# Attention with a mixture-of-experts gate on one core: expert groups cut in half, one per step and ahead of the value matmuls, fewer transfers per head group, weights and biases staged later

## The chip, the cores and the metric

The kernel runs on one core of a Trainium2 chip. The metric is the device time of one execution in microseconds (us); lower is better. The state before is given as the median of three runs. All durations below come from one profiled execution of it.

## What is computed

`x` is 4 sequences of 1024 tokens with 128 features, in float32. After a layer norm the same rows feed two branches, whose product is added to `x`:

```python
xn = _layernorm(x, axis=-1)
s = _L0_attn_ref(xn, Wv, bv, Wo, bo)     # q = k = v = xn @ Wv.T + bv, 16 heads of 8
g = _silu(_L0_ffn_ref(xn, ...))          # second norm, router, top 2 of 8 experts, 128 -> 256 -> 128
x = x + s * g
```

In the attention q, k and v are the same projection, the softmax runs over 1024 keys, and the scale is 1/sqrt(8). In the second branch every token goes to the two experts with the highest router logits (`gelu`, exact form) and the two results are mixed with renormalised weights.

## The kernel before, in words

Every engine has its instructions written out in order; semaphores tie the engines together. The program has a front part, 256 steps, and a short tail.

**Front part.** The 4096 tokens are 32 tiles of 128, in 8 blocks of 4 tiles. VectorE (DVE) makes the norm's statistics (`norm1`, L684 and on), ScalarE (ACT) applies them (L592), TensorE (PE) transposes each block (`turn_x`, L1020), projects it (L1027), makes router logits (L1032), transposes the projection back for the values (`turn_p`, L1040) and sums squares per head (L1046). GpSimd (POOL) splits the projection into a high and a low part (L532 to L537), and the DMA queue of SyncE (SP) stores both parts in `p_dram` (L390) and half the squared norm in `m_dram` (L392). At the end of the front part a branch on the largest norm chooses whether an exact path runs; with these inputs it doesn't.

**The steps.** A unit is 4 heads of one sequence; there are 16 units of 16 steps. A step g is one block of 128 keys against 512 queries, for 4 heads: PE makes the scores in two halves of two heads (L1096, into three PSUM pairs in turn), ACT takes the exponential of each half (L651), and two steps later (`VLAG`) PE multiplies them with the values (L1108) into one PSUM bank, `bank_v`, which collects 8 steps. After each 8 steps, at g = 1 mod 8, `turn_out` on DVE waits for the last value matmuls, transposes `bank_v` (L908), which frees it for the next 8 steps, and then divides by the row sums (L911, L912). `k_ring` and `q_ring` hold the operands of two units; SP loads a unit with 20 transfers (L375 to L383).

**The other work.** Everything else that PE does during the steps goes through one further PSUM bank, `bank_f`: each user ("use") writes it on PE (`write_bank`), and DVE reads it (`read_bank`) before the next use may write. PE waits for `bank_f_read` ahead of a use. The table `USES`, made by `timetable()`, says at which step each use stands: a "turn" and a "project" for each unit (attention output transposed at L1121, output projection L1125), two counts of the router, 40 "up" uses (L1140) and 40 "down" uses (L1150). The experts' tokens are sorted into 80 groups of 128 rows (40 for each half of the tokens, `h`). A quad is four groups; a use holds two groups of a quad, so four 128x128 matmuls. In a step the uses stand last:

```python
scores(g, 0); scores(g, 1)
if g >= VLAG: values(g - VLAG)
for use in USES.get(g, []): write_bank(*use)
```

DVE's order in a step is `turn_out` (where due), the reads of this step's uses, then `beside(g)`: router arithmetic, the transposes of expert inputs (`turn_z`, L888), the mixing (`combine`, L893, L895) and the last products (L902, L903). POOL issues the indirect transfers that scatter the rows to `z_dram` (L548) and gather the results (L564), and stores `o_ring` (L554). SP loads weights into rings of two quads (`load_w1` L440, `load_w2` L451) and the sorted rows (L462) in the order of the step numbers, and waits in that order. The exact gelu (L631) runs once for each half of the tokens on ACT, at the steps `GELU_AT`; the uses of the first two down quads stand together in the step of it ("burst").

The expert work stands at steps 31 to 189, mostly one use in every second step.

Of the kernel before, what the change touches and what calls it, by code (L numbers as in the profile page):

```python
# [16 lines left out]
P = 128  # L17
B, S, D = 4, 1024, 128
H = 16
# [36 lines left out]
KQ_LOADS = PART_LOADS + 4  # L56
XC = 8
# [15 lines left out]
ROUTE_AT = (0, 16)  # L73
SCALE_Z_AT = (5, 22)
EXP_AT = (2, 18)
COUNT_AT = (7, 23)
WEIGH_AT = (13, 29)
SCALE_W1_AT = 10
SCATTER_AT = (13, 30)
MOE_AT = 31  # L80
MOE_STEP = 2.1
GATHER_LAG = 3
COMBINE_LAG = 5


def timetable():
# [15 lines left out]
    def both(kind, q, t):  # L102
        for i in range(2):
            t = max(t, place((kind, q, i), t) + 1 - MOE_STEP) + MOE_STEP
        return t

    def burst(first, t):

        g = int(t) + 2
        while g in uses:  # L110
            g += 1
        uses[g] = [("down", first + k, i) for k in range(2) for i in range(2)]
        at.update({what: g for what in uses[g]})
        return g

    for h in range(HALVES):
        place(("count", h), COUNT_AT[h])
    t = MOE_AT
# [6 lines left out]
    for k in range(2, QUADS):  # L125
# [4 lines left out]
    for k in range(2, QUADS):  # L130
# [7 lines left out]
    gather = [at["down", (h + 1) * QUADS - 1, 1] + GATHER_LAG for h in range(HALVES)]  # L138
# [5 lines left out]
SILU_AT = (GATHER_AT[0] + HT + COMBINE_LAG + 2, min(GATHER_AT[1] + HT + COMBINE_LAG + 2, STEPS))  # L144
# [4 lines left out]
def build(nc, x, Wv, bv, Wo, bo, ln_g, ln_b, rW, rb, W1, b1, W2, b2, out):  # L149
    ctx = ExitStack()  # L150
    with ctx:
# [98 lines left out]
        p_dram = nc.dram_tensor("p_dram", [H, PARTS, DK, N], F32)  # L250
        w1_dram = nc.dram_tensor("w1_dram", [E, P, W1W], F32)
        w2_dram = nc.dram_tensor("w2_dram", [E, P, W2W], F32)
        m_dram = nc.dram_tensor("m_dram", [MPARTS, H, N], F32)
# [3 lines left out]
        x_in = [sem(f"x_in{c}") for c in range(NT // XC)]  # L257
# [44 lines left out]
        w2_kept = sem("w2_kept")  # L302
        logits_mm = sem("logits_mm")
# [38 lines left out]
        def _(sp):  # L342
            def load_x(c):
                sp.dma_start(x_tok[:, c * XC:(c + 1) * XC, :], x_v[:, c * XC:(c + 1) * XC, :]).then_inc(x_in[c], 16)
# [9 lines left out]
            for c in range(1, NT // XC):  # L354
                load_x(c)
            sp.dma_start(rb_bc[:, :], rb.rearrange("(a d) -> a d", a=1).broadcast_to([P, E])).then_inc(small_in, 16)
            sp.dma_start(bo_bc[:, :], bo.rearrange("(a d) -> a d", a=1).broadcast_to([P, D])).then_inc(small_in, 16)
            sp.dma_start(w1_stage, W1.rearrange("e h f -> h e f")).then_inc(w1_staged, 16)
            for c in range(FC):
                sp.dma_start(w2_dram[:, :, c * D:(c + 1) * D], W2[:, c * P:(c + 1) * P, :]).then_inc(w2_kept, 16)  # L360
            for e in range(E):
                sp.dma_start(w2_dram[e, :, FC * D:W2W], b2[e:e + 1, :].broadcast_to([P, D])).then_inc(w2_kept, 16)
            sp.wait_ge(zeros_ready, 1)
            sp.dma_start(m_dram[1, :, :], s_tok[0:H, :, :].rearrange("h t d -> h (t d)")).then_inc(m_zeroed, 16)
# [6 lines left out]
            def load_heads(batch, first_head, slot, loaded):  # L371
                for j in range(4):
                    head = p_dram[bass.ds(first_head + j, 1), :, :, bass.ds(batch * S, S)].rearrange("h a d n -> (h a d) n")
                    first = 32 * j
                    sp.dma_start(k_ring[first:first + DK, slot, :].bitcast(F32), head[0:DK, :]).then_inc(loaded, 16)  # L375
                    sp.dma_start(k_ring[first + DK:first + 3 * DK, slot, :].bitcast(F32), head[:, :]).then_inc(loaded, 16)
                    sp.dma_start(q_ring[first:first + 2 * DK, slot, :].bitcast(F32), head[:, :]).then_inc(loaded, 16)
                    sp.dma_start(q_ring[first + 2 * DK:first + 3 * DK, slot, :].bitcast(F32), head[0:DK, :]).then_inc(loaded, 16)

            def load_stabiliser(n, loaded):  # L380
                for j in range(4):
# [806 lines left out]
```

## Time and profile before

| what | value |
|---|---|
| median of 3 runs | 669.34 us (668.44 to 671.91) |
| the profiled execution | 668.3 us, its span 666.6 us |
| PE matmul busy | 585.1 us (88%), weight load 247.6 us |
| ACT busy | 540.7 us (81%), of it L651: 480.0 us in 512 instructions |
| DVE busy | 222.5 us (33%) |
| POOL busy | 171.3 us (26%) |
| DMA | 77.15 MB, mean 116 GB/s |
| first exponential, last exponential | at 74.4 us, at 656.1 us |

Busy shares are averages over three stages: a front part of 74 us, 582 us of steps, and a tail. An engine that is 88% busy in the mean can be the limit in one stretch and idle for 13 us in another, so the stretches are read apart below. The granted clock of TensorE is one of two levels, 1.2 or 2.4 GHz, shown as tenths of full speed.

### The profile page before, as it was taken

What the parts mean: (1) busy time and instruction counts of PE and PEld (TensorE: products, weight loads), DVE (VectorE), ACT (ScalarE), POOL (GpSimd) and SP (SyncE); (2) the same over time, 40 slices, a digit from 0 to 9 for tenths busy, and PEclk for the clock granted to TensorE, in tenths of its full rate; (3) what the DMA queues carried; (4) which work ended last, traced back from release to release, by engine and by line L of the source; (5) the groups of instructions that cost most, each with busy time, mean ns of one, the idle gap of its engine ahead of it and who ended that gap; (6) DMA issues with size and microseconds to landing.
All of it is one profiled execution on the core that took longest, in us unless ns stands there. A gap on an engine that the chain in (4) does not pass through costs nothing.

```text
span 666.6 us, 11435 instructions
## 1 busy us (share of the span) xinstructions
PE 585.1 (88%) x4002; PEld 247.6 (37%) x4002; DVE 222.5 (33%) x581; ACT 540.7 (81%) x595; POOL 171.3 (26%) x192
## 2 busy tenths in 40 slices
PE   1895599929897997999999999979979899699996
PEld 1673123213343444344444444344434332223231
DVE  5942556613232321222222231224415123321111
ACT  3533599918586889889888989898888799999995
POOL 5435007777600000000000000547300067300000
PEclk9958599959898996999999999969979899989998
DMA  7628335444754453555544453445725241312000
GB/s 217 159 73 301 96 153 165 113 102 137 180 134 110 97 114 97 122 135 137 130 111 122 124 133 91 131 124 148 190 82 160 88 102 52 89 33 58 1 10 8
DMA packets 96212, 77.15 MB, mean 116 GB/s; under 512 B 52723, under 2 KB 86918, under 8 KB 95622
## 3 DMA queue, kind: packets, MB, share of 16 engines
q1 hardware_dynamic: 90454, 62.73, 35.8%
q0 software_dynamic: 5696, 13.64, 7.0%
q8 instruction: 33, 0.54, 0.3%
q14 instruction: 29, 0.24, 0.1%
HBM read 53.77 MB, written 24.13 MB: 117 GB/s over the span
## 4 chain that ended last, share of the span: by engine, by line
PE 60%; ACT 14%; issue 9%; SPq 7%; DMA 4%; DVE 4%; POOL 2%; POOLq 0%; ACTq 0%; DVEq 0%
PE bank_v L1108 27%; PE pair L1096 14%; ACT exps L651 12%; PE bank_f L1150 7%; PE bank_f L1140 6%; POOL rows_in_sb L564 2%; SPq L439 1%; PE bank_f L1125 1%; DVE o_turned L908 1%; DMA rows_in_sb<-o_dram,dest_i 1%; DMA m_dram<-pre 1%; SPq L440 1%; DMA bo_bc<-in_L_attn_bo 1%; SPq L462 1%; PE pair L1027 1%
## 5 line engine op out<-in xcount | busy, mean ns | idle before, releaser
L651 ACT ACTIVATE exps<-pair 128x1024 f32<-128x1024 f32 x512 | 480.0, 1080 | 78.2 <-PE pair L1096 76.7
L1108 PE MATMUL bank_v<-exps,v_tok 128*32 128x512 f32 x2048 | 283.8, 627 | 5.7 <-DVE o_turned L908 3.3
L1096 PE MATMUL pair<-q_ring,k_ring 26*128 26x512 f32 x1024 | 176.5, 514 | 14.5 <-ACT exps L651 8.9
L1096 PEld LDWEIGHTS pair<-q_ring,k_ring 26*128 26x128 f32 x1024 | 76.2, 188 | 177.6 <-ACT exps L651 112.5
L554 POOL DMA_DIRECT2D o_dram<-o_ring x20 | 15.4, 768 | 292.2 <-DVE o_ring L950 288.7
L548 POOL DMA_INDIRECT z_dram<-pre,dest_i x64 | 63.4, 990 | 49.2 <-DVE dest_i L871 30.0
L1108 PEld LDWEIGHTS bank_v<-exps,v_tok 128*32 128x32 f32 x2048 | 41.9, 110 | 72.9 <-issue 56.9
L564 POOL DMA_INDIRECT rows_in_sb<-o_dram,dest_i x64 | 60.8, 950 | 25.5 <-issue 20.1
L1140 PE MATMUL bank_f<-zT,w_ring 128*128 128x128 f32 x320 | 48.5, 298 | 21.3 <-issue 13.2
L1150 PE MATMUL bank_f<-w_ring,pre 128*128 128x128 f32 x320 | 52.8, 315 | 10.8 <-ACT pre L631 5.2
L1140 PEld LDWEIGHTS bank_f<-zT,w_ring 128*128 128x128 f32 x320 | 40.8, 200 | 56.0 <-issue 45.1
L1150 PEld LDWEIGHTS bank_f<-w_ring,pre 128*128 128x128 f32 x320 | 44.5, 216 | 42.2 <-issue 29.6
L941 DVE TENSOR_TENSOR pre<-bank_f,w_ring 128x512 f32<-128x512 f32 x40 | 27.6, 690 | 92.1 <-PE bank_f L1140 92.1
L908 DVE STREAM_TRANSPOSE o_turned<-bank_v 128x512 f32<-128x512 f32 x32 | 22.9, 717 | 103.2 <-PE bank_v L1108 103.0
L950 DVE TENSOR_TENSOR o_ring<-bank_f,w_ring 128x256 f32<-128x256 f32 x40 | 17.0, 424 | 108.2 <-PE bank_f L1150 108.2
L592 ACT ACTIVATE xn_tok<-x_tok,shift,rstd 128x128 f32<-128x128 f32 x32 | 13.0, 480 | 9.5 <-DVE shift L691 9.5
L888 DVE STREAM_TRANSPOSE zT<-z_ring 128x512 f32<-128x512 f32 x20 | 14.2, 710 | 16.2 <-DMA z_ring<-z_dram 15.6
L631 ACT ACTIVATE pre<-pre 128x2048 f32<-128x2048 f32 x10 | 18.2, 1896 | 0.0
L613 ACT ACTIVATE pre<-bank_v 16x512 fp32r<-16x512 f32 x8 | 4.7, 586 | 16.5 <-PE bank_v L1046 9.6
L893 DVE SCALAR_TENSOR_TENSOR xn_tok<-rows_in_sb,weight,xn_tok 128x128 f32<-128x128 f32 x32 | 11.3, 352 | 15.9 <-DMA rows_in_sb<-o_dram,dest_i 15.6
L1020 PE MATMUL pair<-ident,xn_tok 128*128 128x128 f32 x32 | 8.4, 415 | 8.8 <-ACT xn_tok L592 8.8
L926 DVE TENSOR_TENSOR s_tok<-bank_f,bo_bc 128x256 f32<-128x256 f32 x16 | 6.8, 424 | 27.5 <-PE bank_f L1125 27.5
(129 smaller groups left out, 296.1 us busy)
## 6 DMA issues: line engine op xcount, KB each, us to landing
w_ring<-w_dram SPq DMA_DIRECT2D x80, 192.0 KB
w_ring<-w_dram SPq DMA_DIRECT2D x80, 129.0 KB
z_dram<-s_tok SPq DMA_DIRECT2D x4, 1280.0 KB, 6.6
z_ring<-z_dram SPq DMA_DIRECT2D x80, 64.0 KB, 2.4
o_dram<-o_ring POOLq DMA_DIRECT2D x20, 256.0 KB, 3.2
p_dram<-pre SPq DMA_DIRECT2D x16, 256.0 KB, 3.2
k_ring<-p_dram SPq DMA_DIRECT2D x64, 64.0 KB
q_ring<-p_dram SPq DMA_DIRECT2D x64, 64.0 KB
```

The lines of the kernel that those rows point to most:

```text
L548: pool.indirect_dma_start(z_dram[h][:, :], bass.IndirectOffsetOnAxis(dest_i[:, h, c, i:i + 1].bitcast(U32), 0), z0[:, h * HT + i, :], None ...
L554: pool.dma_start(o_dram[h][k * 4 * P:(k + 1) * 4 * P, :].rearrange("(a p) d -> p a d", p=P), o_ring[:, q % 2, :, :]).then_inc(o_stored[q % ...
L564: pool.indirect_dma_start(rows_in_sb[:, (h * HT + i) % GATHER_RING, c, :], None, o_dram[h][:, :], bass.IndirectOffsetOnAxis(dest_i[:, h, c ...
L631: nc.scalar.activation(part, part, ACT.Gelu).then_inc(gelu_done, 1)
L651: nc.scalar.activation(exps[:, g % ES, 2 * half:2 * half + 2, :], pair[(2 * g + half) % 3][:, :, :], ACT.Exp, scale=SCALE).then_inc(exp_do ...
L908: nc.vector.transpose(o_turned[:, qh, :, :], bank_v[:, :].rearrange("p (r s) -> p s r", s=QR)).then_inc(o_turned_ready, 1)
L941: ins = nc.vector.tensor_tensor(pre[:, k, i * BLK:(i + 1) * BLK].rearrange("p (s c t) -> p s c t", s=2, c=FC), bank_f[:, :].rearrange("p ( ...
L950: ins = nc.vector.tensor_tensor(o_ring[:, q % 2, 2 * i:2 * i + 2, :], bank_f[:, 0:2 * D].rearrange("p (a d) -> p a d", a=2), w2_ring[:, q ...
L1096: ins = nc.tensor.matmul(pair[h % 3][:, j % 2, :], k_ring[32 * j:32 * j + KROWS, n % 2, kt * P:(kt + 1) * P], q_ring[32 * j:32 * j + KROWS ...
L1108: ins = nc.tensor.matmul(bank_v[32 * j:32 * j + 32, :], v_tok[:, (n // HG) * KT + kt, first:first + 32], exps[:, g % ES, j, :], start=(kt ...
L1140: ins = nc.tensor.matmul(bank_f[:, at * P:(at + 1) * P], w1_ring[:, q % 2, a, c * P:(c + 1) * P], zT[:, q % 2, a * P:(a + 1) * P], start=T ...
L1150: ins = nc.tensor.matmul(bank_f[:, (a % 2) * D:(a % 2 + 1) * D], pre[:, k, (a * FC + c) * P:(a * FC + c + 1) * P], w2_ring[:, q % 2, a, c ...
```

## The change

It does eight things.

- A use holds one group: two matmuls in place of four. There are 160 expert uses, up and down, with a new table; outside the bursts nearly every step from 31 to 217 has one. A burst has eight.
- In a step that has exactly one use, PE now writes it between the scores and the value matmuls. In a burst it still comes last. This holds for turn, project and count too.
- `p_dram` holds for each head the rows high, high, low, high, norm, zero (two of them filled by a copy in DRAM at step 2), so that a unit from the third on is loaded with 8 transfers, not 20. The first two units are loaded as before; the first unit's loads are spread over four blocks.
- The 16 small bias matmuls of W1 leave the front part and become four "bias" uses at steps 4 to 7.
- PE does 9 and 8 matmuls of the identity into `bank_v` ahead of the first block (`keep_warm`). The norm's first chunks are smaller, and DVE keeps block 0's values ahead of the last chunk. The loads of `rb` and `bo` aren't waited for there any more.
- The zeroing of `z_dram` moves behind the branch (first half) and to step 16 (second half); the copy of W2 and b2 into DRAM moves from the start to step 24 of SP's queue.
- The router arithmetic and the scatter stand earlier: the first scatter at step 6 (13 before), the second at 22 (30 before).
- `store_o` moves from POOL's queue to SP's, and `combine` takes 7 steps for 5 tiles in place of 5.

```diff
-ROUTE_AT = (0, 16)
-SCALE_Z_AT = (5, 22)
-COUNT_AT = (7, 23)
-SCALE_W1_AT = 10
-SCATTER_AT = (13, 30)
+RANK_AT = ((0, 0, 1, 1, 2, 2), (13, 14, 15, 16, 18, 19))
+COUNT_AT = (3, 20)
+ASSIGN_AT = ((3, 4, 4, 5, 6), (21, 22, 23, 24, 26))
+SCALE_Z_AT = ((3, 4, 5, 6), (14, 15, 16, 18))
+BIAS_AT = 4
+SCALE_W1_AT = (8, 10, 11, 12)
+SCATTER_AT = (6, 22)
 MOE_AT = 31
-MOE_STEP = 2.1
+MOE_STEP = 1.12
...
     def both(kind, q, t):
-        for i in range(2):
+        for i in range(4):
...
             def load_unit(n):
                 if n >= 2:
                     sp.wait_ge(pv_done, (n - 1) * US)
-                load_heads(n // HG, (n % HG) * 4, n % 2, kq_in[n % 2])
-                load_stabiliser(n, kq_in[n % 2])
+                if n == 2:
+                    sp.wait_ge(hi_copied, 32)
...
+                    sp.dma_start(k_ring[32 * j:32 * j + PROWS, n % 2, :].bitcast(F32), p_dram[head, 0:PROWS, tokens]
+                                 ).then_inc(kq_in[n % 2], 16)
+                    sp.dma_start(q_ring[32 * j:32 * j + KROWS, n % 2, :].bitcast(F32), p_dram[head, HI_ROW:HEAD_ROWS, tokens]
+                                 ).then_inc(kq_in[n % 2], 16)
...
+            zero_z(0)
             load_unit(1)
-            zero_z(1)
...
+                if g == SCATTER_AT[1] - 6:
+                    zero_z(1)
+                if g == SCATTER_AT[1] + 2:
+                    keep_w2()
                 for q in range(HALVES * QUADS):
-                    if g == (TURN_Z_AT[q - 2] + 1 if q >= 2 else SCATTER_AT[0] + HT - 1):
+                    if g == (TURN_Z_AT[q - 2] + 1 if q >= 2 else MOE_AT - 3):
                         load_z(q)
-                    if g == (AT["up", q - 2, 1] + 1 if q >= 2 else SCATTER_AT[0] + 9 + q):
+                    if g == (AT["up", q - 2, 3] + 1 if q >= 2 else MOE_AT - 8 + 2 * q):
                         load_w1(q)
...
-            norm1(0, 0, XC)
+            norm1(0, *NORMS[0])
+            norm1(1, *NORMS[1])
             router_weights()
-            norm1(1, XC, XC)
-            norm1(2, 2 * XC, 2 * XC)
+            norm1(2, *NORMS[2])
             keep_p(0)
+            norm1(3, *NORMS[3])
+            keep_p(1)
+            keep_p(2)
...
-                    for a in range(2 * i, 2 * i + 2):
-                        for c in range(FC):
-                            at = (a % 2) * FC + c
-                            ins = nc.tensor.matmul(bank_f[:, at * P:(at + 1) * P], w1_ring[:, q % 2, a, c * P:(c + 1) * P],
-                                                   zT[:, q % 2, a * P:(a + 1) * P], start=True, stop=True)
+                    for c in range(FC):
+                        ins = nc.tensor.matmul(bank_f[:, c * P:(c + 1) * P], w1_ring[:, q % 2, i, c * P:(c + 1) * P],
+                                               zT[:, q % 2, i * P:(i + 1) * P], start=True, stop=True)
...
+                ahead = len(USES.get(g, [])) == 1
+                if ahead:
+                    write_bank(*USES[g][0])
                 if g >= VLAG:
                     values(g - VLAG)
-                for use in USES.get(g, []):
-                    write_bank(*use)
+                if not ahead:
+                    for use in USES.get(g, []):
+                        write_bank(*use)
```

How rows move, on PE. Steps 41 and 42 of the program; L1140 (before) and L1191 (now) write the expert uses, L1096 and L1142 the scores, L1108 and L1154 the value matmuls. Before, from the scores of step 41:

```order
L1096 MATMUL pair<-q_ring,k_ring 128x512 x4
L1108 MATMUL bank_v<-exps,v_tok 32x512 x4
L1140 MATMUL bank_f<-zT,w_ring 128x128 x4
L1096 MATMUL pair<-q_ring,k_ring 128x512 x4
L1108 MATMUL bank_v<-exps,v_tok 32x512 x4
```

Now, from the second use of the two, with the semaphores:

```order
L1191 MATMUL bank_f<-zT,w_ring 128x128
L1154 MATMUL bank_v<-exps,v_tok 32x512 [waits exp_done]
L1154 MATMUL bank_v<-exps,v_tok 32x512 x3
L1142 MATMUL pair<-q_ring,k_ring 128x512 [waits exp_done]
L1142 MATMUL pair<-q_ring,k_ring 128x512
L1142 MATMUL pair<-q_ring,k_ring 128x512 [waits exp_done]
L1142 MATMUL pair<-q_ring,k_ring 128x512
L1191 MATMUL bank_f<-zT,w_ring 128x128 [waits bank_f_read]
L1191 MATMUL bank_f<-zT,w_ring 128x128
L1154 MATMUL bank_v<-exps,v_tok 32x512 [waits o_turned_ready,exp_done]
L1154 MATMUL bank_v<-exps,v_tok 32x512 x3
```

The last value matmuls of an 8-step block now stand behind step 41's use and ahead of step 42's, which waits for `bank_f_read`; before, step 42 had no use.

On DVE, around the same place. L888 and L926 are `turn_z`, L908 to L912 and L946 to L950 `turn_out`, L941 and L981 the reads of the up uses. Before:

```order
L888 STREAM_TRANSPOSE zT<-z_ring 128x512
L941 TENSOR_TENSOR pre<-bank_f,w_ring 128x512
L908 STREAM_TRANSPOSE o_turned<-bank_v 128x512
L911 RECIPROCAL rden<-o_turned 128x16
L912 TENSOR_TENSOR attn<-o_turned,rden 128x128
L941 TENSOR_TENSOR pre<-bank_f,w_ring 128x512
L888 STREAM_TRANSPOSE zT<-z_ring 128x512
```

Now:

```order
L926 STREAM_TRANSPOSE zT<-z_ring 128x512
L946 STREAM_TRANSPOSE o_turned<-bank_v 128x512
L949 RECIPROCAL rden<-o_turned 128x16
L950 TENSOR_TENSOR attn<-o_turned,rden 128x128
L981 TENSOR_TENSOR pre<-bank_f,w_ring 128x256 x4
L926 STREAM_TRANSPOSE zT<-z_ring 128x512
```

The reads are half as wide and twice as many, and in both the read of the use of step 41 stands behind the three instructions of `turn_out`.

## Rows read from the trace of the kernel before

**Rows 1.** Chain of work that ended last, late steps: start us, us, what.

```profile
592.08 1.67 ACT exps L651 x2
593.88 1.70 ACT exps L651 x2
```

**Rows 2.** Timeline, PE, two expert uses: start us, us, engine, line, operation.

```profile
303.75 1.16 PE L1150 MATMUL bank_f<-w_ring,pre 128*128 128x128 f32 x8
304.84 0.51 PE L1096 MATMUL pair<-q_ring,k_ring 26*128 26x512 f32 x4
305.28 1.06 PE L1108 MATMUL bank_v<-exps,v_tok 128*32 128x512 f32 x8
306.28 0.69 PE L1096 MATMUL pair<-q_ring,k_ring 26*128 26x512 f32 x4
307.89 1.16 PE L1150 MATMUL bank_f<-w_ring,pre 128*128 128x128 f32 x8
```

**Rows 3.** Groups by form: scatter; timeline: what waited for it.

```profile
L548 POOL DMA_INDIRECT z_dram<-pre,dest_i x64 | 63.4, 990 | 49.2 <-DVE dest_i L871 30.0 <-issue 19.2
...
145.57 0.71 DVE L888 STREAM_TRANSPOSE zT<-z_ring 128x512 f32<-128x512 f32 x1 [15.60 <-DMA z_ring<-z_dram]
```

**Rows 4.** Waits, 150 to 250 us: us in total, times, longest us.

```profile
PE bank_f L1140 <- DMA w_ring<-w_dram: 7.9, 3, 3.5
```

**Rows 5.** Page, part 2: granted clock of PE in 40 slices, tenths.

```profile
PEclk9958599959898996999999999969979899989998
```

**Rows 6.** Timeline, PE, a project use (two matmuls) and the scores after it.

```profile
609.27 0.71 PE L1125 MATMUL bank_f<-woT,attnT 128*128 128x128 f32 x4
609.91 0.51 PE L1096 MATMUL pair<-q_ring,k_ring 26*128 26x512 f32 x4
```

**Rows 7.** Timeline at the end of 8 steps; last, groups by form, a 256-wide read.

```profile
170.69 1.16 PE L1140 MATMUL bank_f<-zT,w_ring 128*128 128x128 f32 x8
170.90 0.72 DVE L908 STREAM_TRANSPOSE o_turned<-bank_v 128x512 f32<-128x512 f32 x1 [2.45 <-PE bank_v L1108]
172.15 0.68 DVE L941 TENSOR_TENSOR pre<-bank_f,w_ring 128x512 f32<-128x512 f32 x1
...
L926 DVE TENSOR_TENSOR s_tok<-bank_f,bo_bc 128x256 f32<-128x256 f32 x16 | 6.8, 424 | 27.5 <-PE bank_f L1125 27.5
```

**Rows 8.** Timeline, PE, second and third down use of the first burst.

```profile
257.86 2.08 PE L1150 MATMUL bank_f<-w_ring,pre 128*128 128x128 f32 x8 [0.52 <-DVE o_ring L950]
260.52 2.08 PE L1150 MATMUL bank_f<-w_ring,pre 128*128 128x128 f32 x8 [0.59 <-DVE o_ring L950]
```

**Rows 9.** Timeline, SP's queue: W2 and b2 copied to DRAM at the start.

```profile
9.49 6.41 SPq L360 DMA_DIRECT2D w_dram<-in_L_ffn_W  x2
...
15.94 7.42 SPq L362 DMA_DIRECT2D w_dram<-in_L_ffn_b  x8
```

**Rows 10.** Chain of work that ended last, front part.

```profile
31.95 4.99 PE bank_f L1011 x32
...
59.59 6.88 DMA m_dram<-pre
```

**Rows 11.** Timeline, PE, sum of squares of four blocks: two slow turns, two fast.

```profile
42.42 0.60 PE L1046 MATMUL bank_v<-pre,head_sel 128*16 128x512 bf16 x1
...
48.15 0.60 PE L1046 MATMUL bank_v<-pre,head_sel 128*16 128x512 bf16 x1
...
52.57 0.38 PE L1046 MATMUL bank_v<-pre,head_sel 128*16 128x512 bf16 x1
...
55.61 0.38 PE L1046 MATMUL bank_v<-pre,head_sel 128*16 128x512 bf16 x1
```

**Rows 12.** Timeline, DVE: norm of the last 16 tiles, and what follows it.

```profile
19.76 3.19 DVE L684 BATCH_NORM_STATS2 rows_in_sb<-x_tok 128x6 f32<-128x128 f32 x16
...
29.07 0.69 DVE L707 COPY v_tok<-pair 128x512 f32<-128x512 f32 x1
```

**Rows 13.** Groups by form: one of the router's wide comparisons.

```profile
L808 DVE TENSOR_TENSOR pre<-pre 128x1024 bf16<-128x1024 f32 x2 | 2.4, 1222 | 0.0
```

More of the change, by code:

```diff
@@ L111, in burst @@
             g += 1
-        uses[g] = [("down", first + k, i) for k in range(2) for i in range(2)]
+        uses[g] = [("down", first + k, i) for k in range(BURST) for i in range(4)]
         at.update({what: g for what in uses[g]})
@@ L117, in timetable @@
         place(("count", h), COUNT_AT[h])
+    for part in range(4):
+        place(("bias", part), BIAS_AT + part)
     t = MOE_AT
@@ L124, in timetable @@
     t = both("up", QUADS + 1, t)
-    for k in range(2, QUADS):
+    for k in range(BURST, QUADS):
         t = both("down", k, t)
@@ L129, in timetable @@
     t = gelu[1] + 4
-    for k in range(2, QUADS):
+    for k in range(BURST, QUADS):
         t = both("down", QUADS + k, t)
@@ L137, in timetable @@
             order[what] = len(order)
[L138 removed]
+    gather = [at["down", (h + 1) * QUADS - 1, 3] + GATHER_LAG for h in range(HALVES)]
     return uses, at, order, gelu, gather
@@ L476, in _ @@
                     load_unit(n + 1)
-                if g == SCALE_W1_AT + 6:
+                if g == 2:
+                    for row in (0, LO_ROW + DK):
+                        sp.dma_start(p_dram[:, row:row + DK, :], p_dram[:, HI_ROW:HI_ROW + DK, :]).then_inc(hi_copied, 16)
+                if g == SCALE_W1_AT[-1] + 1:
                     sp.wait_ge(w1_scaled, 1)
@@ L571, in _ @@
                         scatter(h, g - SCATTER_AT[h])
-                for q in range(HALVES * QUADS):
-                    if g == AT["down", q, 1] + 1:
-                        store_o(q)
                 for h in range(HALVES):
@@ L681, in norm1 @@
                 for t in range(count):
-                    if (first + t) % XC == 0:
-                        dve.wait_ge(x_in[(first + t) // XC], 16)
+                    for chunk, (start, _) in enumerate(X_CHUNKS):
+                        if first + t == start:
+                            dve.wait_ge(x_in[chunk], 16)
                     ins = nc.vector.bn_stats(stats[:, t, :], x_tok[:, first + t, :])
@@ L782, in scale_w1 @@
                     dve.wait_ge(w1_staged, 16)
-                    dve.wait_ge(biases_mm, 1)
+                    dve.wait_ge(bank_f_written, written("bias", 3))
                 some = slice(2 * part, 2 * part + 2)
@@ L928, in read_bank @@
                                                   bo_bc[:, :].unsqueeze(1).broadcast_to([P, UT, D]), ALU.add)
+                elif what == "bias":
+                    some = slice(arg[0] * 4, arg[0] * 4 + 4)
+                    ins = nc.vector.tensor_tensor(b1p[:, some], bank_f[:, 0:4], cols[:, some], ALU.add)
                 elif what == "count":
@@ L996, in _, with keep_warm @@
             pe.wait_ge(consts_ready, 8)
+            def keep_warm(count):
+                for _ in range(count):
+                    nc.tensor.matmul(bank_v[:, 0:P], ident[:, :], ident[:, :], start=True, stop=True)
+            keep_warm(WARM[0])
             pe.wait_ge(rows_in, 16 * 6)
@@ L1126, in write_bank @@
                                                start=True, stop=True)
+                elif what == "bias":
+                    if arg[0] == 0:
+                        pe.wait_ge(w1_staged, 16)
+                    for at in range(4):
+                        e, c = divmod(arg[0] * 4 + at, FC)
+                        ins = nc.tensor.matmul(bank_f[:, at:at + 1], w1_stage[:, e, c * P:(c + 1) * P],
+                                               cols[:, E * FC + 1:E * FC + 2], start=True, stop=True)
                 elif what == "count":
```

234 lines of the change are left out of this document (124 added, 110 removed).

## The prediction

> **What bounds the kernel now.** I read the page first for the clock, then the chain of waits, then timelines of single steps, because the busy shares average over stretches with different limits. Late in the run, where no expert work is left, the chain stays on ACT and a pair of exponentials starts every 1.80 us [rows 1]: ACT bounds those steps at 1.81 us. Where expert uses stand in every second step, PE bounds. Two steps take 307.89 - 303.75 = 4.14 us, and the timeline splits them: the use 1.09, scores 0.44, values 1.00, scores again up to the next use 1.61 with values [rows 2]. So a step with a whole use costs PE 0.44 + 1.00 + 1.09 = 2.53, a step without one 1.44, below ACT's 1.81; together the pair loses 4.14 - 3.61 = 0.53 us against ACT. Between steps 31 and about 60 the limit is neither: PE stands at its queue's head for sorted rows or weights [rows 3, 4]. The granted clock falls to the lower of its two levels (1.2 GHz) in the front part, after the gap for the rows and at both gelus, the slices with 5 or 6 tenths [rows 5].
>
> **The sum, part by part.** It is made against the profiled execution's 668.3 us; the median of the runs shown is 1.0 higher. All terms are changes of that time.
>
> *Half uses.* Two fp32 matmuls of 128x128 into `bank_f` are what a project use is: 609.91 - 609.27 = 0.64 us [rows 6]. A step with a half use then takes PE 0.44 + 0.64 + 1.00 = 2.08, which is 0.27 over ACT's 1.81. Outside the bursts there are 144 half uses: 144 x 0.27 = 39. Before there were 72 whole ones at 0.53: 38. So cutting the groups in half brings nothing by itself, because the fixed part of a use, 2 x 0.64 - 1.09 = 0.19, is paid twice and eats what the better balance gives. Term: 0. Bounds: no row shows a use between scores and values. At 0.55 (half of 1.09) it would be -13, at 0.73 +13. I take 0.64, the row with the same shape.
>
> *The place ahead of the values.* This is the largest loss. At g = 1 mod 8 DVE has to do `turn_out` before it reads that step's use. `turn_out` waits for the value matmuls, which now stand behind the use. After the values end on PE (170.69) the transpose starts 0.21 later, and the read of the use 1.46 later; a read 256 wide takes 0.42 [rows 7]; with 0.06 for the semaphore (what the 0.58 between two burst uses leaves beside read and its start [rows 8]) PE may write the next use 1.94 us after the values' end. PE has only the scores of the next step, 0.44, to do meanwhile, and its own value matmuls are queued behind the waiting use, the next scores behind those, and ACT behind the scores. So it stands for 1.5 us. With the use behind the values, scores and values (1.44) and the use of the step before (0.64) would have covered it. In the new table 21 ends of 8 steps have one use in both steps. At three of them (steps 49, 97, 137) a `turn_z` of 0.71 [rows 3] follows that read, and the next use, the first of its quad, waits for it too. 21 x 1.5 + 3 x 0.7 = +33.6. What it gives back: the value matmuls that open a new 8 steps waited for the transpose (0.21 + 0.72 + 0.06 after the end, scores cover 0.44: 0.55) where a use made PE late, in 8 steps before: -4. ACT has 0.27 to spare a step in this stretch, but it is PE that is late, so nothing is recovered.
>
> *Bursts.* Each use there waits for the read of the one before: start to start 260.52 - 257.86 = 2.66, of which 0.58 is the handshake, at the lower clock [rows 8]. Eight half uses take 8 x (1.04 + 0.5) = 12.3, four whole ones 10.6. PE already finished after the gelu, so the end shows: +1.7 to +2.6 twice, +4.5.
>
> *The scatter.* First use before: POOL issues 32 indirect transfers for half the tokens at (63.4 + 19.2) / 64 = 1.29 us each, 41 us; DVE waited 15.6 us for sorted rows, and PE and ACT behind it [rows 3]. Now it starts about 7 steps (12.6 us) earlier, and step 31 comes some 3 us later, so the rows come in time by POOL. But SP's queue is passed differently: W2's and b2's copy stands at step 24, between the W1 loads and the rows' loads. [...] Behind it are four W1 loads and the row loads. I leave 4 us of stall: -11. Bounds: -15 (copy hidden), 0 (SP as late as POOL was).
>
> *Weight waits.* PE waited three times for W1, 7.9 us in all [rows 4], each time with a unit's 20 transfers ahead of the loads on SP, and PE's matmuls behind two of them run at the lower clock. Eight transfers take less than half. With the slow steps behind the waits I put this at -12; bounds -15 and -3 (three waits become short ones). `store_o` on SP adds one issue for each quad; there is room.
>
> *Front part.* The 32 records of the bias matmuls, 4.99 us, leave the chain, and so does the 6.88 us wait for a store that stood behind the zeroing of `z_dram` [rows 10]. A loop over a block took 5.73 us at the lower clock and 3.04 at the higher [rows 11], and the clock fell during the bias matmuls. Against that, DVE now takes block 0's values ahead of the last 16 tiles' norm, 29.07 - 19.76 = 9.3 us of work [rows 12]. The block's sum of squares is there at 26 to 28.6 us by its own loops, so blocks 4 to 7 start at 37 to 40 us, with PE idle before them, in place of about 37 with PE busy (42.42 less a loop). Term -8, bounds -13 and +4. The trace shows the loops up to 51 us at 1.2 GHz, behind the thinly loaded bias matmuls, and those from 52 us at 2.4 [rows 11]. The Trainium skill (TensorE: Matmul & The Clock Gate, What's actually happening) says the default state is throttled and activity releases it; by that the extra identity matmuls bring the higher level sooner, and with it kept for all blocks the term would be -13. The gap ahead of block 4 speaks against its being kept.
>
> *First steps.* Steps 0 to 8 now hold all of the first routing and four bias uses. The wide comparisons are 1.22 us each [rows 13]; with the routing's small ones I estimate 2.4 us of DVE work a step against 1.81. PE waits at the count and bias uses: +3 (0 to +6).
>
> *Late stretch.* Slower gathering (7 steps for 5 tiles) avoids DVE waits ahead of reads, and a step behind a free one has 0.2 us in hand: -4 (0 to -6). The gathers of the second half start at step 220 and have 36 steps, 65 us, for 41 us of POOL's work, so the tail stays. Nothing for the 8-transfer units beyond the above: bytes are equal.
>
> Sum: 0 + 33.6 - 4 + 4.5 - 11 - 12 - 8 + 3 - 4 = +2 us, so 670 by the profiled run. I take 669, as the gains' bounds reach a little further than the losses'.
>
> **Rivals.**
>
> 1. *The wait at the end of 8 steps is mostly covered.* If DVE's read came soon enough, or most of these places found PE early, half of the 33 us goes: about 650. For it: only DVE timings of before stand behind the 1.94. Against: no use was written there before, and the order on both engines is fixed. 0.15.
>
> 2. *A use ahead of the values costs less.* If its weights are loaded while the scores still stream, only the pieces are left, (1.09 - 0.64) / 4 = 0.11 each, 0.45 in all: 144 x 0.19 = -27, about 642. The trace speaks against it: each change between forms leaves a gap, and the step's 0.64 has it [rows 2, 6]. The Trainium skill (TensorE: Matmul & The Clock Gate, Step-by-step: what each phase is for) has the queue pull weight loads ahead of matmuls in flight where row groups don't conflict. 0.08.
>
> 3. *Slower: SP's queue.* If the copy at step 24 keeps SP beyond step 31, the first rows and the second W1 quad come late, PE idles over 3 us, and its clock falls. It decides from about 10 us for the copy. With the full 13.8 us the stall is about as long as before [rows 3, 9]: +11 and +4 for the clock, about 684. 0.15.
>
> 4. *Slower: the handshake shows in all steps.* Uses in every step leave DVE one step for the read and everything beside it. If `beside` delays reads by 0.3 us in most steps, 144 x 0.3 = +43, about 710. Against: DVE is 33% busy. 0.05.
>
> **How the numbers follow.** My case has 0.57, with bounds of its own terms from 659 to 681; a third of it is over 0.5% faster (about what a measurement of this kernel can tell from no change), a third within, a third slower. Faster: 0.19 + 0.15 + 0.08 = 0.42; same 0.19; slower 0.19 + 0.15 + 0.05 = 0.39. The range leaves out the far ends of rivals 2 and 4: 650 to 686.
>
> **What would show it.** In the profile after: steps with a half use 2.08 us apart; at steps 42, 50, 58, ... 3.6 us, with PE's weight load of the use waiting about 1.5 us for DVE's read of the use before; some 21 such waits. The scatter's wait of 15 us gone and at most 5 us at step 31; no wait over 1 us for W1; first exponential at 66 us (61 to 78). Bursts of about 12 us. I am wrong if step 42 and its like take 2.1 us, if half uses run at 1.9 us, or if SP issues the first row loads later than step 31.

## The result, and the profile after

The changed kernel takes 689.41 us (median of 4 runs, 689.14 to 696.62), the kernel before, run beside it, 670.62 us (4 runs, 668.44 to 674.79). The ratio is 1.0298, with an interval from 1.0213 to 1.0384: slower, and above the forecast range. The profiled execution took 689.35 us with a span of 687.4, so 20.8 us of span have to be found. Where one execution took over 1.5% longer than the fastest of its kernel, the ratio leaves it out; that is one number below, the 660.3 of the first experiment.

A step's length is read here as the distance between the first exponential of one step and of the next, and its excess as what it has over ACT's 1.81 us. Summed by stretch, the excess of the two profiled executions differs as below. Two rows are made otherwise: the ends of 8 steps are what the changed kernel's 21 steps take over a usual step with a use (2.07), and "all else" is what is left of the difference.

| stretch | term of the prediction | measured |
|---|---|---|
| up to the first exponential (74.4 before, 70.9 now) | -8 | -3.5 |
| steps 3 to 8 | +3 | +13.1 |
| steps 9 to 30 | 0 | +0.4 |
| step 31, first sorted rows | -11 | -7.1 |
| 21 ends of 8 steps | +33.6 | +33.3 |
| the two gelus with their bursts | +4.5 | +5.1 |
| the two silus (ACT, L671), five steps each | none | +1.6 |
| all else from step 32 on: 0 for half uses, -4 value waits, -12 weights, -4 late stretch | -20 | -22.1 |
| sum | +2 | +20.8 |

The page of the profile after, cut to its first line, the clock of part 2 (tenths, 40 slices) and one of the costliest groups (busy us, mean ns, idle before and who released it):

```profile
PE 592.3 (86%) x4036; PEld 245.9 (36%) x4036; DVE 238.0 (35%) x677; ACT 547.6 (80%) x595; POOL 155.1 (23%) x172
...
PEclk9677559979999997699999999999789989999977
...
L1191 PE MATMUL bank_f<-zT,w_ring 128*128 128x128 f32 x320 | 58.3, 306 | 25.1 <-DVE pre L981 14.8
```

Before, the low tenths of the clock stood at the front, behind the gap at step 31 and at the gelus [rows 5]; now slices 5 and 6 (69 to 103 us) are low as well, where the first steps run. And the up uses now have a wait that they had not: PE stood 14.8 us for DVE's read of the use before.

**One end of 8 steps.** The timeline of the program's step 42 (start us, us; PEld is the weight load), from the last value matmuls of the old 8 steps:

```profile
173.01 1.06 PE L1154 MATMUL bank_v<-exps,v_tok 128*32 128x512 f32 x8
174.01 0.51 PE L1142 MATMUL pair<-q_ring,k_ring 26*128 26x512 f32 x4
174.15 0.72 DVE L946 STREAM_TRANSPOSE o_turned<-bank_v 128x512 f32<-128x512 f32 x1 [1.86 <-PE bank_v L1154]
174.90 0.25 DVE L949 RECIPROCAL rden<-o_turned 128x16 f32<-128x16 f32 x1
175.18 0.29 DVE L950 TENSOR_TENSOR attn<-o_turned,rden 128x128 f32<-128x128 f32 x1
175.39 0.42 DVE L981 TENSOR_TENSOR pre<-bank_f,w_ring 128x256 f32<-128x256 f32 x1
175.87 0.52 PEld L1191 LDWEIGHTS bank_f<-zT,w_ring 128*128 128x128 f32 x4 [1.67 <-DVE pre L981]
175.87 0.71 PE L1191 MATMUL bank_f<-zT,w_ring 128*128 128x128 f32 x4 [1.35 <-DVE pre L981]
176.51 1.06 PE L1154 MATMUL bank_v<-exps,v_tok 128*32 128x512 f32 x8
177.50 0.19 PEld L1142 LDWEIGHTS pair<-q_ring,k_ring 26*128 26x128 f32 x4 [0.84 <-issue]
...
178.05 1.94 ACT L686 ACTIVATE exps<-pair 128x1024 f32<-128x1024 f32 x2 [1.56 <-PE pair L1142]
```

The transpose starts when the values have ended, the read (L981) comes third behind it, and PE, with only 0.5 us of scores left to do, waits 1.35 us. Behind it stand the value matmuls, behind those the next scores, and ACT waits 1.56 us for them. Most other steps with a use are 2.05 to 2.08 us long. Of the 21 with this wait 18 take 3.36 to 3.57, two 4.19 and 4.20, where `turn_z` follows, and step 50, where `turn_z` follows too and the clock fell, 5.76. (Step 178, without a use in the step before it, takes 3.07 and isn't one of them.) Before, the same place had the transpose, a whole read and no use behind it [rows 7].

**Step 31.** SP's queue, then DVE, and PE:

```profile
128.00 2.33 SPq L377 DMA_DIRECT2D w_dram<-in_L_ffn_W  x2
130.38 8.09 SPq L379 DMA_DIRECT2D w_dram<-in_L_ffn_b  x8
139.68 3.65 SPq L468 DMA_DIRECT2D w_ring<-w_dram  x4
143.37 6.75 SPq L490 DMA_DIRECT2D z_ring<-z_dram  x12
...
147.48 0.71 DVE L926 STREAM_TRANSPOSE zT<-z_ring 128x512 f32<-128x512 f32 x1 [9.04 <-DMA z_ring<-z_dram]
...
148.30 1.19 PE L1191 MATMUL bank_f<-zT,w_ring 128*128 128x128 f32 x4 [6.12 <-issue]
```

The copy at step 24 held SP for 10.5 us, the second W1 quad another 3.7, and so the row loads were first issued at 143.37, behind the start of step 31 (about 142). The step took 9.9 us, where the wait for rows had been 15.60 [rows 3]. In the kernel before the same copy took 6.41 + 7.42 us [rows 9].

**Steps 4 to 7.** PE, two of the four bias uses (L1178), with scores and values:

```profile
80.37 0.80 PE L1142 MATMUL pair<-q_ring,k_ring 26*128 26x512 f32 x4
81.10 1.87 PE L1178 MATMUL bank_f<-cols,w_ring 128*128 128x1 f32 x8
82.90 1.93 PE L1154 MATMUL bank_v<-exps,v_tok 128*32 128x512 f32 x8
84.76 0.80 PE L1142 MATMUL pair<-q_ring,k_ring 26*128 26x512 f32 x4
85.49 1.86 PE L1178 MATMUL bank_f<-cols,w_ring 128*128 128x1 f32 x8
```

PE's rows lie end to end: nothing waits. But scores take 0.73 and values 1.86 from start to start, where they take 0.44 and 1.00 at 2.4 GHz [rows 2], and the four fp32 matmuls of one column (eight records) cost 1.80. A step is 4.39 us, four times over. The granted clock was at the lower level from 64.3 us to 101.8, so up to the step after the last bias use.

### The profile page after: what moved, and what is told of

It reads as the page before. It is cut to its first block and busy times, and to the rows that moved or that the text cites. A ratio compares the mean times of both kernels' runs of the same rounds, so it can differ in the third digit from the quotient of the medians.

```text
span 687.4 us, 11510 instructions
## 1 busy us (share of the span) xinstructions
PE 592.3 (86%) x4036; PEld 245.9 (36%) x4036; DVE 238.0 (35%) x677; ACT 547.6 (80%) x595; POOL 155.1 (23%) x172
## 5 line engine op out<-in xcount | busy, mean ns | idle before, releaser
L686 ACT ACTIVATE exps<-pair 128x1024 f32<-128x1024 f32 x512 | 487.6, 1049 | 93.7 <-PE pair L1142 77.8
L1154 PE MATMUL bank_v<-exps,v_tok 128*32 128x512 f32 x2048 | 287.2, 634 | 2.3 <-DVE o_turned L946 1.6
L1142 PE MATMUL pair<-q_ring,k_ring 26*128 26x512 f32 x1024 | 157.1, 519 | 14.4 <-ACT exps L686 8.7
L1142 PEld LDWEIGHTS pair<-q_ring,k_ring 26*128 26x128 f32 x1024 | 62.4, 190 | 250.1 <-ACT exps L686 193.3
L1200 PE MATMUL bank_f<-w_ring,pre 128*128 128x128 f32 x320 | 64.8, 331 | 24.3 <-DVE o_ring L990 16.3
L1191 PE MATMUL bank_f<-zT,w_ring 128*128 128x128 f32 x320 | 58.3, 306 | 25.1 <-DVE pre L981 14.8
L946 DVE STREAM_TRANSPOSE o_turned<-bank_v 128x512 f32<-128x512 f32 x32 | 22.9, 717 | 133.3 <-PE bank_v L1154 133.3
L981 DVE TENSOR_TENSOR pre<-bank_f,w_ring 128x256 f32<-128x256 f32 x80 | 33.9, 424 | 97.8 <-PE bank_f L1191 97.8
L1200 PEld LDWEIGHTS bank_f<-w_ring,pre 128*128 128x128 f32 x320 | 48.1, 216 | 46.7 <-DVE o_ring L990 22.7
L990 DVE TENSOR_TENSOR o_ring<-bank_f,w_ring 128x128 f32<-128x128 f32 x80 | 23.2, 291 | 107.8 <-PE bank_f L1200 106.9
L1191 PEld LDWEIGHTS bank_f<-zT,w_ring 128*128 128x128 f32 x320 | 43.1, 195 | 45.9 <-issue 23.2
L1154 PEld LDWEIGHTS bank_v<-exps,v_tok 128*32 128x32 f32 x2048 | 41.6, 110 | 46.6 <-issue 20.9
L627 ACT ACTIVATE xn_tok<-x_tok,shift,rstd 128x128 f32<-128x128 f32 x32 | 13.1, 480 | 12.8 <-DVE shift L727 12.8
L926 DVE STREAM_TRANSPOSE zT<-z_ring 128x512 f32<-128x512 f32 x20 | 14.2, 711 | 9.7 <-DMA z_ring<-z_dram 9.0
L575 POOL TENSOR_TENSOR pre<-pre 128x512 bf16<-128x512 f32 x8 | 8.3, 1041 | 31.5 <-ACT pre L642 25.1
L956 DVE COPY attnT<-bank_f 128x256 f32<-128x256 f32 x16 | 6.8, 425 | 22.2 <-PE bank_f L1167 22.2
```

What stands on the lines that cost most here:

```text
L686: nc.scalar.activation(exps[:, g % ES, 2 * half:2 * half + 2, :], pair[(2 * g + half) % 3][:, :, :], ACT.Exp, scale=SCALE).then_inc(exp_do ...
L926: nc.vector.transpose(zT[:, q % 2, :], z_ring[:, q % 2, :]).then_inc(z_turned, 1)
L946: nc.vector.transpose(o_turned[:, qh, :, :], bank_v[:, :].rearrange("p (r s) -> p s r", s=QR)).then_inc(o_turned_ready, 1)
L981: ins = nc.vector.tensor_tensor(pre[:, k, i * HF:(i + 1) * HF].rearrange("p (c t) -> p c t", c=FC), bank_f[:, 0:HF].rearrange("p (c t) -> ...
L990: ins = nc.vector.tensor_tensor(o_ring[:, q % 2, i, :], bank_f[:, 0:D], w2_ring[:, q % 2, i, FC * D:W2W], ALU.add)
L1142: ins = nc.tensor.matmul(pair[h % 3][:, j % 2, :], k_ring[32 * j:32 * j + KROWS, n % 2, kt * P:(kt + 1) * P], q_ring[32 * j:32 * j + KROWS ...
```

## Experiments

Each was run with a profile and timed against the kernel before on the same chip. Ratios are to the kernel before; the changed kernel stands at 1.0298.

**Uses behind the values again**, all else as changed:

```diff
-ahead = len(USES.get(g, [])) == 1
+ahead = False
```

> Every use stands behind the value matmuls, as before; all else as in the change. Theory A (the wait at the ends of 8 steps): the 21 steps behind such an end fall from 3.4 to 3.6 us (4.2 and 5.8 at three) to about 2.1, the waits of PE for DVE's read of the use before are gone, other steps with a half use stay at 2.07; 689.4 - 33 = 656 us. Theory B (the place costs nothing, half uses in nearly every step are what costs): within 3 us of 689. Should the value matmuls that open 8 steps wait for the transpose again, up to 21 x 0.5 = 10 us come back: 666.

Measured 649.46 us (648.34 to 660.3) against 669.59, ratio 0.9705 (0.9632 to 0.9778): one line turns the loss into a gain. The place of step 42 in this kernel:

```profile
163.44 0.72 DVE L946 STREAM_TRANSPOSE o_turned<-bank_v 128x512 f32<-128x512 f32 x1 [0.23 <-PE bank_v L1154]
...
164.38 1.07 PE L1154 MATMUL bank_v<-exps,v_tok 128*32 128x512 f32 x8
...
165.37 0.71 PE L1191 MATMUL bank_f<-zT,w_ring 128*128 128x128 f32 x4
```

PE comes to that use with its values done, and the read is done too; step 42 takes 2.06 us. From step 32 on the excess falls from 121.1 to 90.2 us, by 31.0, which is about the 33.3 less the small value waits that come back. The other 10 us are not the place itself: step 31 is 2.6 shorter, and steps 3 to 16 together 7.5, because here the bias uses met the higher clock:

```profile
81.64 1.06 PE L1154 MATMUL bank_v<-exps,v_tok 128*32 128x512 f32 x8
82.64 1.05 PE L1178 MATMUL bank_f<-cols,w_ring 128*128 128x1 f32 x8
...
87.47 1.15 PE L1178 MATMUL bank_f<-cols,w_ring 128*128 128x1 f32 x8
88.55 0.80 PE L1142 MATMUL pair<-q_ring,k_ring 26*128 26x512 f32 x4
89.28 1.94 PE L1154 MATMUL bank_v<-exps,v_tok 128*32 128x512 f32 x8
```

The same use takes 0.98 instead of 1.80 from start to start, steps 4 to 6 take 2.42, and at the fourth use the clock falls; steps 8 to 10 are then 2.6 to 2.9 long.

**Which of two steps is to blame.** At an end of 8 steps two steps are involved: g = 1 mod 8 brings `turn_out` and its own use ahead of the last values, g = 2 mod 8 brings the use that waits. One kernel each puts only that step's use behind the values (`VLAG` is 2, `KT` is 8):

```diff
-ahead = len(USES.get(g, [])) == 1
+ahead = len(USES.get(g, [])) == 1 and g % KT != VLAG
```

> As the change, but in the steps g = 2 mod 8, and only there, the use stands behind the value matmuls. Theory A: the same 656 to 666 us as with all uses behind, since the place costs only there. Theory B: 689. If the place costs in every step, this one lies between 689 and the run with all uses behind.

```diff
-ahead = len(USES.get(g, [])) == 1
+ahead = len(USES.get(g, [])) == 1 and g % KT != 1
```

> As the change, but in the steps g = 1 mod 8, and only there, the use stands behind the values. By the chain read from DVE: after the values' end PE has the use (0.64) and scores (0.44) to do and may write the next use at 1.94, so it waits 0.86, not 1.5, in each of 21 places: 689.4 - 21 x 0.64 = 676 us, the steps g = 2 mod 8 at about 2.9. If the wait is something else than the read behind turn_out, 689 or 656.

The first took 673.86 us (10 runs; 1.0062, 1.0031 to 1.0094), the second 674.24 (10 runs; 1.0077, 1.0049 to 1.0106). Each recovers 15 us and leaves the other half; for the second that was forecast, for the first 656 to 666 us had been. In the first, the values that open the new 8 steps wait for the transpose, and the use behind them makes step 43 late too: steps 42 and 43 take 2.64 and 2.30.

```profile
174.70 0.72 DVE L946 STREAM_TRANSPOSE o_turned<-bank_v 128x512 f32<-128x512 f32 x1 [1.86 <-PE bank_v L1154]
...
175.57 1.07 PE L1154 MATMUL bank_v<-exps,v_tok 128*32 128x512 f32 x8 [0.49 <-DVE o_turned L946]
```

In the second the last value matmuls don't stand behind a use of 0.64 us, but the use of step 42 still waits (the row below), and the step takes 2.85.

```profile
173.78 0.71 PE L1191 MATMUL bank_f<-zT,w_ring 128*128 128x128 f32 x4 [0.71 <-DVE pre L981]
```

So the wait is one chain, values, transpose, read, next use, and what counts is how much of PE's work stands between its two ends: scores alone (0.44) in the change, scores and one more piece in these two, scores, values and a use (2.08) when both stand behind.

**Bias uses later.**

```diff
-BIAS_AT = 4
-SCALE_W1_AT = (8, 10, 11, 12)
+BIAS_AT = 9
+SCALE_W1_AT = (13, 14, 15, 16)
```

> The four bias uses stand at steps 9 to 12 (4 to 7 in the change), the scaling of W1 at 13 to 16. Theory C (four thin uses at the lower clock, each 1.8 us, keep that clock down): steps 4 to 8 return to 1.82, the clock rises by about step 5 and the bias uses, then at the higher level, cost 2.4 to 2.5 a step; 689.4 - 10 = 679 us. Theory D (the clock stays down until about 100 us whatever PE does, or DVE's routing work sets those steps): steps 4 to 8 stay over 3 us, less than 3 us gained.

Measured 689.13 us (685.53 to 690.38), ratio 1.0289 (1.022 to 1.0359): a miss, nothing gained. Steps 4 to 8 ran at 1.81 to 1.84, with the clock up at 84 us, but then the steps of the bias uses took 2.27, 3.88, 4.38 and 4.39:

```profile
92.16 1.05 PE L1178 MATMUL bank_f<-cols,w_ring 128*128 128x1 f32 x8
...
95.73 1.05 PE L1178 MATMUL bank_f<-cols,w_ring 128*128 128x1 f32 x8 [1.09 <-DVE b1p L969]
96.71 1.07 PE L1154 MATMUL bank_v<-exps,v_tok 128*32 128x512 f32 x8
97.71 0.80 PE L1142 MATMUL pair<-q_ring,k_ring 26*128 26x512 f32 x4
98.44 1.86 PE L1178 MATMUL bank_f<-cols,w_ring 128*128 128x1 f32 x8
```

The clock was up, two bias uses ran on it, and it fell at 97.7. Of the 3.88 us of step 10, 1.09 are a wait for DVE, whose read stands behind `turn_out`. The loss goes where the uses go, so the crowding of the first steps is not its cause.

**Bias uses with 128 columns.** The same four matmuls multiply a copy of the bias column, repeated 128 times (`b_wide`); DVE reads the first column of each.

```diff
-ins = nc.tensor.matmul(bank_f[:, at:at + 1], ..., cols[:, E * FC + 1:E * FC + 2], ...)
+ins = nc.tensor.matmul(bank_f[:, at * P:(at + 1) * P], ..., b_wide, ...)
```

> As the change, but each of the 16 bias matmuls moves 128 equal columns, not one (column 0 is read); same places, same number of instructions. Theory C (thin matmuls keep the clock down): the clock rises by about step 5, steps 5 to 7 take about 2.5, not 4.39, and 8 to 11 stay at 1.82: 689.4 - 8 = 681 us. Theory G (transfers or the routing keep steps 4 to 7 slow, at 84 to 88% DMA share): the steps stay at 4.4 or grow by the wider matmuls, 689 or more.

```profile
83.78 2.08 PE L1178 MATMUL bank_f<-rows_in_sb,w_ring 128*128 128x128 f32 x8
...
87.59 1.16 PE L1178 MATMUL bank_f<-rows_in_sb,w_ring 128*128 128x128 f32 x8
```

At the lower clock the wide use costs more (2.01 from start to start), but the clock rose at 86.6, within its step, and stayed: 3.81, then 2.52 three times. The excess of steps 3 to 8 is 5.6 us, not 13.3. The whole, 685.63 us (682.38 to 687.6; 1.0221, 1.0166 to 1.0276), can't be told apart from the change by these intervals, and the front part of its profiled execution was 3.4 us longer; the verdict rests on the steps. The other runs bear it out: steps 5 to 7 take 2.51 to 2.53 us in all six kernels with wide bias uses, and 4.39 in all four that have one-column uses there ahead of the values. In the Trainium skill, TensorE: Matmul & The Clock Gate (What's actually happening) says that the throttled state is the default and activity releases it. The sentence alone doesn't tell these two cases apart: TensorE's rows lie end to end in both, and with one-column matmuls among them the clock stayed at 1.2 GHz for four steps, with wide ones it rose in the first.

**W2's copy at step 8 of SP's queue.**

```diff
-if g == SCATTER_AT[1] + 2:
+if g == SCATTER_AT[0] + 2:
     keep_w2()
```

> W2 and b2 are copied to DRAM at step 8 of SP's queue, not 24. Theory E (at step 31 the sorted rows wait for SP's queue, which stands in that copy): the row loads are issued at about 131 us, not 143, step 31 takes about 2 us, not 9.9, the clock stays up; 689.4 - 8 = 681 us. Theory F (the scatter itself is late): step 31 stays over 8 us, no gain.

Measured 682.2 us (681.45 to 685.0), ratio 1.0208 (1.0145 to 1.0271). Step 31 is 2.06 us long; its excess goes from 8.09 to 0.25. That is the whole of the stall, so here SP alone was late: its row loads went out at 131.43, and POOL had issued the last scatter of the first half by 129.8.

**The three together**, behind the values, wide bias, early copy:

> All uses behind the values, the W2 copy at step 8, and the right side of the bias matmuls 128 equal columns wide in place of one (column 0 of each is read). If the three costs are separate: 649.5 - 7 (step 31) - 4 (steps 4 to 11, where the run with all uses behind still had a slow stretch) = 638 us. If they cover one another: no less than 645.

Measured 649.91 us (647.85 to 651.05), ratio 0.9709 (0.9667 to 0.975): no better than the first edit alone (638 had been forecast if the three costs are separate). Step 31 is clean, but step 26 takes 7.88. The copy now holds SP for 23.7 us, and the zeroing of `z_dram`'s second half (L384) stands behind it; DVE's output of the first project waits for it:

```profile
85.81 14.87 SPq L377 DMA_DIRECT2D w_dram<-in_L_ffn_W  x2
100.72 8.82 SPq L379 DMA_DIRECT2D w_dram<-in_L_ffn_b  x8
...
111.12 3.12 SPq L384 DMA_DIRECT2D z_dram<-s_tok  x2
```

and from its waits (us in total, times, longest):

```profile
DVE s_tok L964 <- DMA z_dram<-s_tok: 7.9, 1, 7.9
```

**And the zeroing ahead of the copy** ("mended" from here on):

```diff
-if g == SCATTER_AT[1] - 6:
+if g == 4:
     zero_z(1)
```

> As the run with three mends, and the second half of z_dram is zeroed at step 4 of SP's queue, ahead of the W2 copy. There the copy held back that zeroing, and DVE's read of the first projection waited 7.9 us for it. Without it: 649.9 - 7 = 643 us, no step below 31 over 3 us from step 8 on. If another transfer behind the copy is late instead: 648 to 650.

Measured 648.01 us (6 runs, 646.21 to 650.58), ratio 0.9693 (0.9667 to 0.9718). Step 26 is clean, and the stall is at step 31 again, 7.9 us of excess:

```profile
DVE zT L926 <- DMA z_ring<-z_dram: 10.8, 1, 10.8
```

Step 31 comes sooner, at 132.9 us, by what the earlier stretches saved, and SP is late again, by a third path. SP's queue, a wait of SP in it (us in total, times, longest), and POOL's 32nd scatter, the last that these rows need:

```profile
87.33 20.55 SPq L377 DMA_DIRECT2D w_dram<-in_L_ffn_W  x2
...
116.94 0.74 SPq L517 DMA_DIRECT2D w_dram<-b1p  x1
...
127.32 8.31 SPq L468 DMA_DIRECT2D w_ring<-w_dram  x8
135.68 6.90 SPq L490 DMA_DIRECT2D z_ring<-z_dram  x12
...
SPq L463 <- DMA w_dram<-b1p: 2.4, 1, 2.4
...
128.54 1.08 POOL L592 DMA_INDIRECT z_dram<-pre,dest_i  x1 [0.30 <-issue]
```

The copy now holds SP for 28.9 us. The store of W1's bias behind it lands at 126.2, the eight W1 loads wait for that, and the row loads go out behind them without a wait for POOL. By POOL alone they could have gone out at about 130.9, an estimate from the kernel before, where they did so 1.3 us after the 32nd scatter had ended (140.41 and 141.72). So some 4.8 of the 7.9 us are SP's, and POOL would be the next to be late. That is the other forecast of this run, another transfer behind the copy that is late (648 to 650 us). No run here moves the copy behind the row loads.

**The last 16 tiles' norm ahead of block 0's values**, on the mended kernel:

```diff
-            keep_p(0)
             norm1(3, *NORMS[3])
+            keep_p(0)
```

> As the mended kernel, but DVE makes the norm of the last 16 tiles before it keeps block 0's values, as the kernel before did. In the change, PE stood idle for 5.6 us ahead of block 4, at 38.4 us. If that order is what kept the front part long, block 4 starts at about 31 to 33 us and the first exponential comes 4 to 7 us earlier: 637 us. If the slow clock or the stores set the front part's length: within 2 us of the mended kernel.

Measured 645.73 us (6 runs, 643.24 to 647.46), ratio 0.9649 (0.9619 to 0.9678), the lowest median here and ahead of both kernels; the gain over the mended kernel, 2.3, is less than the 4 to 7 forecast, and the two intervals touch. The first exponential is at 67.5 instead of 71.4, and step 31 gives 1.2 back.

**Twenty transfers for each unit again**, on the mended kernel:

```diff
-KQ_LOADS = 4 * 2
+KQ_LOADS = KQ_FIRST
```

and `load_unit` loads every unit as it loads unit 1.

> As the mended kernel, but each unit is loaded with 20 transfers, as before. If they cause the waits for W1 before: 5 to 13 us slower, with waits of PE for w_ring at steps 38 to 60. If the new table's spacing alone took those waits away: within 2 us.

Measured 656.28 us (6 runs, 655.05 to 656.98), ratio 0.9802 (0.9778 to 0.9825), 8.3 over the mended kernel. Its profiled execution loses 10.4, of it 5.6 in steps 32 to 78, and there PE waits for weights three times, where the mended kernel shows one wait of 1.1:

```profile
PE bank_f L1191 <- DMA w_ring<-w_dram: 3.7, 3, 1.8
```

**Whole groups again**, on the mended kernel, one in every second step:

```diff
-MOE_STEP = 1.12
+MOE_STEP = 2.1
...
-        for i in range(4):
+        for i in range(2):
```

with four matmuls to a use and reads twice as wide, as before.

> As the mended kernel, but with whole uses (two groups, four matmuls) at the places of the kernel before, one in every second step. From the step lengths half uses bring nothing by themselves (144 x 0.27 against 72 x 0.53) and lose about 5 us in the bursts: this run at 636 to 643 us, no more than 3 us from the mended one or a little below. If cutting the groups is a gain: over 650.

Measured 654.01 us (6 runs, 650.09 to 655.89), ratio 0.977 (0.974 to 0.98), 6.0 over the mended kernel: a miss, since at most 3 had been forecast, and over 650 us if cutting the groups is a gain. The steady rate is not the reason: a step without and a step with a whole use take 1.82 + 2.31 = 4.13, two half uses 2 x 2.075 = 4.15. It loses more at single places, the largest a late quad of weights at step 60 (6.51 us long against 3.22 in the mended kernel, with the lower clock in the two behind it):

```profile
PE bank_f L1196 <- DMA w_ring<-w_dram: 2.9, 1, 2.9
```

**The kernel before with its single uses ahead of the values:**

```diff
+ahead = len(USES.get(g, [])) == 1
+if ahead: write_bank(*USES[g][0])
 if g >= VLAG: values(g - VLAG)
-for use in USES.get(g, []): write_bank(*use)
+if not ahead:
+    for use in USES.get(g, []): write_bank(*use)
```

> The kernel before with whole uses, in which a single use of a step is written ahead of the values; nothing else. Theory A: the place costs only where two neighbouring steps around an end of 8 steps have uses; before, that is one place (steps 33, 34 have it not, nearly all ends have one use), and the value matmuls that open 8 steps no longer wait for the transpose, 8 x 0.5: 670 - 4 = 666 us. If the place costs in general: over 680.

Measured 675.77 us (10 runs, 673.13 to 678.94), ratio 1.0088 (1.0055 to 1.0121): a miss, I had expected no loss. With a use in every second step most ends of 8 steps cost little (about 0.25 us at seven of them), and where the opening values had waited for the transpose a step even gained some 0.4 us. But where a use is not ready, matmuls that are ready now stand behind it:

```profile
170.11 2.05 PE L1140 MATMUL bank_f<-zT,w_ring 128*128 128x128 f32 x8 [3.80 <-DMA w_ring<-w_dram]
172.09 1.94 PE L1108 MATMUL bank_v<-exps,v_tok 128*32 128x512 f32 x8
```

Step 39 took 8.44 us, not 4.03, and step 56 10.01, not 6.66. The first of these was got back, since steps 43 to 45 together were 5.0 shorter; of the second 1.1 was. Steps 31, 106 and 114 lost 1.9, 1.0 and 2.1 more. At steps 106 and 114 the use, first of its quad, waited 1.6 for DVE's `turn_z`, which stands behind `turn_out` and so behind the end of the values.

## Why the prediction was wrong

It forecast 669 us and no change; the sum was +2 and 20.8 came. The direction was missed by terms on the side, not by the main one.

- **The step that failed is "First steps: +3 (0 to +6)".** It counted DVE's work and PE's waits, and put PE's own time for the four bias uses, and the clock behind it, at nothing. They took 1.80 us each, and the clock stayed at its lower level through them, which made the scores and values of four steps dearer as well: +13.1. The wait for DVE that I expected is there too, in step 3 alone (3.99 us). The two runs that move and widen the bias uses show the uses themselves as the cause: late ones carry the loss with them, wide ones shed 7.7 of the 13.1 us. I had read the same 32 records in the front part as 4.99 us [rows 10] and had even noted that the clock fell there, and then credited their removal and did not charge their return.
- **"The scatter: -11" was too large; it is -7.1.** The place was right, and rival 3 is its mechanism: the copy held SP for 10.5 us, just over the 10 from which it was to decide, and the first row loads were issued later than step 31, a sign of being wrong that the prediction names. The early copy shows that all of the remaining stall was this. My 4 us were 8.1.
- **"Front part: -8" came to -3.5.** PE stood 5.55 us ahead of block 4, as forecast, behind the last 16 tiles' norm. Moving that norm ahead brought the first exponential 3.9 us forward in one profiled execution and the median down by 2.3, and the higher clock was not kept for all blocks.
- **The silus were left out**, +1.6 us. The first costs 7.5 us of excess in five steps in both kernels (from step 171 before, 197 now). The second costs 7.4 against 5.8; behind it the clock was low for 10.2 us against 6.8. Why, no run shows.
- **The place ahead of the values was right**: +33.6 forecast, +33.3 measured, 3.5 us for step 42, PE waiting 1.35 where I had 1.5. Rival 1 is out. Its removal gave 31.0 us from step 32 on, where 33.6 - 4 = 29.6 follows from the terms.
- **Half uses at 2.08 us** were right, so rivals 2 and 4 are out, and "0" for the cut holds for the steady rate (4.15 against 4.13). But whole groups lose 6.0 us, at single waits, and by the run's own test that is a gain of the cut. That these come from the grouping, and not from how this table happens to fall, isn't shown.
- **Bursts** +5.1 for +4.5; **weights and the rest** -22.1 for -20, and this one is a remainder, not a sum of measured parts. Steps 39, 43 to 45, 56 and 58, the long ones before with W1 late [rows 4], have no counterpart now, and the twenty transfers bring waits of the same kind back.

With 13.1 in place of 3 the forecast would have been about 679 us, within the range; SP's queue (3.9), the front part (4.5) and the silus (1.6) make up the other 10. Open is why the clock was up at the bias uses in the first experiment and not in the change: both have the same work up to step 3 but for the place of the values. The four kernels with the one-column uses of steps 4 to 7 ahead of the values all ran them at the lower level; only one kernel has them behind, profiled once, and that doesn't settle whether it is the order or chance.

## What to carry to other kernels

When a wait is moved into an in-order queue, don't ask how long it is but how much of that engine's ready work stands between the event that starts it and the instruction that waits: here one line that put a use ahead of the value matmuls cut that cover from 2.08 us to 0.44, and taking it back won 31 us. Charge an instruction that is moved for what it did where it stood, its effect on the clock included. And after a stall is removed look for the queue that is late next: this one went from step 31 to step 26 and back to 31, each time behind the same copy in SP's queue and each time by another transfer that stood behind it. Moving the copy earlier made it longer and put more behind it.

## What the runs showed of the hardware

- One-column fp32 matmuls cost far more than their columns. A bias use of four took 0.98 us at 2.4 GHz and 1.80 at 1.2, when an up use, two matmuls of 128 columns, took 0.64 at 2.4 GHz. The granted clock fell behind two such uses that ran at the higher level in one kernel and during the fourth in another, and did not rise in the four kernels where they ran at the lower.
- SP's time for one and the same copy in DRAM (W2 and b2) depends on where it stands: 13.8 us at the start, 10.5 at step 24 in the change and 10.8 in the first experiment, 23.7 at step 8 in two kernels, and 28.9 and 30.3 there with the zeroing ahead of it (mended, norm first). The mean busy share of the DMA engines was 0.67 meanwhile in the change, 0.84 in the mended kernel. Whatever is queued behind pays that.
- A transfer that carries no data of the computation can still set the pace: the zeroing of a buffer, queued behind that copy, stopped DVE for 7.9 us.
